# Second attention's loop in a decoder layer: another order of the PSUM banks and of GpSimd's work between its scatters

## The reference, cut to what matters

```
x = LN(x + linear_attention(x))             # 16 heads, elu + 1
x = LN(x + cross_attention(x, ctx_1024))    # 77 context rows a sequence, one head
x = LN(x + ffn(x))
```

```
h = x + proj(attention(LN1(x)))             # "second attention"
z = LN2(h)
gate = softmax(z @ router.T);  top_probs, top_idx = top_k(gate, 2)
out = h + sum over the token's two experts of top_prob * gelu(z @ w1[e]) @ w2[e]
```

## Time and profile before

| what | value |
|---|---|
| plain runs | 758.51, 765.23, 766.54 us; median 765.23 us |
| the profiled execution | 768.66 us, its span 766.9 us |
| busy share of the span | PE 85%, DVE 69%, ACT 51%, POOL 40% |
| mean granted clock of TensorE | 0.922 |

### The profile page before, as it was taken

One profiled execution on the slowest core, in us unless ns is written; L12 is line 12 of the kernel. 1 busy time (PEld: TensorE's weight loads), 2 busy tenths in 40 slices (PEclk: granted clock), 3 DMA queues, 4 the chain that ended last, 5 costly groups with the idle time before them and its releaser, 6 DMA issues.

```text
span 766.9 us, 19226 instructions
## 1 busy us (share of the span) xinstructions
PE 650.8 (85%) x5188; PEld 543.5 (71%) x5189; DVE 530.9 (69%) x1852; ACT 388.7 (51%) x921; POOL 309.5 (40%) x439
## 2 busy tenths in 40 slices
PE   6899999999962889888865319999999999999890
PEld 4679989988841667766655218888888888888540
DVE  1358788788752766888875757777777777777482
ACT  1345656666536656655543605555555555555143
POOL 0246776776631002566658731222222222322141
PEclk9899999999975999999976558999999999999995
DMA  6334434434311000111112331222222222222864
GB/s 203 90 106 130 134 92 141 135 96 119 99 22 28 2 3 2 44 57 57 52 49 71 111 99 50 71 81 69 72 80 69 73 79 69 76 76 63 318 233 133
DMA packets 47709, 68.13 MB, mean 89 GB/s; under 512 B 10576, under 2 KB 34512, under 8 KB 47664
## 3 DMA queue, kind: packets, MB, share of 16 engines
q1 hardware_dynamic: 39080, 46.01, 20.2%
q0 software_dynamic: 6480, 17.87, 6.3%
q10 hardware_dynamic: 2104, 3.68, 1.6%
HBM read 40.21 MB, written 23.12 MB: 83 GB/s over the span
## 4 chain that ended last, share of the span: by engine, by line
PE 54%; DVE 15%; issue 9%; POOL 8%; ACT 4%; DMA 2%; another core or an unknown queue 1%; SPq 1%; POOLq 0%; DVEq 0%; ACTq 0%
PE half_bank L145 9%; PE half_bank L147 9%; PE half_bank L146 9%; PE half_bank L1947 5%; PE half_bank L1475 3%; POOL at_rstd L456 3%; PE half_bank L1928 2%; PE half_bank L1399 2%; PE at_p_q_s L784 1%; POOL shared_x_lo L461 1%; DVE region_prob L1267 1%; DVE ba_top L1264 1%; DVE region_en_small L155 1%; DVE region_h_rows L1289 1%; PE at_p_kv L145 1%
## 5 line engine op out<-in xcount | busy, mean ns | idle before, releaser
L1755 POOL DMA_INDIRECT results<-all_w_qkv,ex_home x71 | 68.2, 960 | 212.3 <-DVE all_w_qkv L1891 183.3
L1788 ACT ACTIVATE region_hid_hi<-half_bank 128x256 fp32r<-128x256 f32 x142 | 46.9, 381 | 79.6 <-PE half_bank L1947 79.5
L145 PE MATMUL half_bank<-region_w_hi,region_hid_hi 128*128 x284 | 81.5, 287 | 1.1 <-DVE region_hid_lo L1883 1.1
L969 POOL DMA_INDIRECT dispatched<-all_xh,all_slot_u x64 | 66.6, 1040 | 36.0 <-DVE all_slot_u L1341 19.0
L146 PE MATMUL half_bank<-all_w,region_hid_hi 128*128 x284 | 79.9, 281 | 0.0
L147 PE MATMUL half_bank<-region_w_hi,region_hid_lo 128*128 x284 | 79.6, 280 | 0.0
L1891 DVE TENSOR_SCALAR all_w_qkv<-half_bank,ex_gate 128x256 f32<-128x256 f32 x71 | 34.3, 484 | 48.0 <-PE half_bank L147 47.5
L1775 ACT ACTIVATE all_xh<-half_bank,all_ln_b,all_ln_w 128x128 f32<-128x128 f32 x142 | 57.7, 466 | 19.5 <-PE half_bank L1928 19.5
L145 PE MATMUL half_bank<-region_w_hi,region_x_hi 128*128 x142 | 63.0, 444 | 0.5 <-DVE region_x_lo L1876 0.5
L1782 ACT ACTIVATE all_w_proj<-half_bank 128x512 f32<-128x512 f32 x71 | 42.5, 598 | 40.2 <-PE half_bank L147 40.2
L145 PEld LDWEIGHTS half_bank<-region_w_hi,region_hid_hi 128*128 128x128 f32 x284 | 53.4, 188 | 11.9 <-issue 8.9
(11 more groups left out here) (258 smaller groups left out, 1822.6 us busy)
## 6 DMA issues: line engine op xcount, KB each, us to landing
all_xh<-dispatched SPq DMA_DIRECT2D x71, 130.5 KB
all_w<-in_moe_w_dram SPq DMA_DIRECT2D x32, 256.0 KB, 3.1
region_y_first<-results SPq DMA_DIRECT2D x12, 512.0 KB, 10.7
all_resid<-at_x SPq DMA_DIRECT2D x32, 128.5 KB
shared_x_t<-in_x_t_dram SPq DMA_DIRECT2D x16, 256.0 KB, 4.2
at_x_tok<-in_x_dram SPq DMA_DIRECT2D x16, 256.0 KB, 4.2
out_dram<-all_w ACTq DMA_DIRECT2D x4, 512.0 KB
ck_ctx_t<-in_ctx_t_dram SPq DMA_DIRECT2D x4, 308.0 KB, 7.2
```

The costliest lines, as they stand in the source:

```text
L145: nc.tensor.matmul(out, a_hi, b_hi, start=(start and i == 0), stop=False)
L969: nc.gpsimd.indirect_dma_start(out=dram["dispatched"], out_offset=bass.IndirectOffsetOnAxis(ap=keep["slot_u"][g % SENDS][:, u, k:k + 1], a ...
L1755: nc.gpsimd.indirect_dma_start(out=dram["results"], out_offset=bass.IndirectOffsetOnAxis(ap=home[par][:, 0:1], axis=0), in_=ym[par], in_of ...
L1788: nc.scalar.activation(hid_hi[par][:, cs, :], p_t[half], ACT.Copy).then_inc(s["hid_high"], 1)
```

## The change

The list of the banks puts the queries before kv, and x before p. `send_rows` and `scatter` take numbers 0 to 7 (tile and expert together) in place of tiles. GpSimd's turn becomes: wait until the second bank of this turn's scores is full, five scatters, residual, one scatter, root, two scatters. What follows the last turn is unchanged but for the numbers.

```diff
-def send_rows(nc, dram, keep, g, tiles):
-
-    for u in tiles:
-        for k in range(2):
+def send_rows(nc, dram, keep, g, numbers):
+
+    for number in numbers:
+        for u, k in (divmod(number, 2),):
             nc.gpsimd.indirect_dma_start(
...
     for n in range(-2, GROUPS + 1):
-        for what, g, parts in (("s", n, 2), ("kv", n + 1, 1), ("q", n + 1, 2), ("p", n, 2), ("x", n + 2, 2), ("o", n, 2),
+        for what, g, parts in (("s", n, 2), ("q", n + 1, 2), ("kv", n + 1, 1), ("x", n + 2, 2), ("p", n, 2), ("o", n, 2),
                                ("v", n + 1, 2), ("a", n, 2), ("h", n - 1, 2)):
...
-        def scatter(g, tiles):
+        def scatter(g, numbers):
             wait_apart(pool, s["slots_ready"], g + 1)
-            send_rows(nc, dram, keep, g, tiles)
+            send_rows(nc, dram, keep, g, numbers)
...
         for n in range(1, GROUPS):
             if there(n - 3):
-                scatter(n - 3, range(0, 3))
-            root(n - 1)
+                bank_of.wait_full(pool, "s", n, 1)
+                scatter(n - 3, range(0, 5))
             residual(n - 1)
             if there(n - 3):
-                scatter(n - 3, range(3, NI))
-        scatter(GROUPS - 3, range(0, 3))
+                scatter(n - 3, range(5, 6))
+            root(n - 1)
+            if there(n - 3):
+                scatter(n - 3, range(6, 2 * NI))
+        scatter(GROUPS - 3, range(0, 6))
         root(GROUPS - 1)
-        scatter(GROUPS - 3, range(3, NI))
-        scatter(GROUPS - 2, range(NI))
-        scatter(GROUPS - 1, range(NI))
+        scatter(GROUPS - 3, range(6, 2 * NI))
+        scatter(GROUPS - 2, range(2 * NI))
+        scatter(GROUPS - 1, range(2 * NI))
         residual(GROUPS - 1)
```

## The result

The changed kernel took 761.39 us (median, 759.62 to 765.58) where the kernel before took 764.72 us in the same series: a ratio of 0.9968, 95% interval [0.9953, 0.9983]. The medians of the 20 runs each lie 3.3 us apart. The ratio with its interval is the measure used here, and by it the change is worth 2.4 us, 1.3 to 3.6 us. The forecast was 5.8 us less (759.4 us). The sign and the range were right, the size was not.

A forecast was written before the change was run, and what follows sets the result against it. A chain of waits was taken to bound each turn of the second attention's loop, with a late release to ScalarE in turns with scatters. 765.23 - (1.1 + 0 + 0.7 + 0.2 + 3.8 + 0 = 5.8) = 759.4 us; range 755.0 to 768.0.

The forecast's parts named there:

- Turn 0 and the banks: Second attention's loop, turn 0: outputs no longer wait for VectorE to free the kv bank, 1.1 us gained.
- The residual: GpSimd's adds leave VectorE's compares, 1.9 us of stretch per turn, for keys and values; worth nearly nothing alone.
- Root: GpSimd's root, which waits for VectorE's variance, just fits in the new order: cost 0, at most 0.5 us.
- Turns 4 to 6, 1.27 us each: Release of TensorE's turned probabilities to ScalarE follows the scatter train, so comes 1.27 us sooner per turn; 3.8 us.
- The rule that the release comes 0.6 us behind the last scatter: Turn 5: the late release before ScalarE's copy comes 0.6 us after the last of six back-to-back scatters.
- The release that stays where it is: Rival: late release unmoved, turns 4 to 6 give nothing; 2.0 us gained, 763.2 us; chance 0.35 with the do-nothing rival.
- That of the kv bank: Rival: delay comes from TensorE standing before the kv bank, new banks end it; 7.9 us gained, 757.3 us; chance 0.2.
- That of a release that waits for the sixth scatter: Rival: release waits for the sixth scatter, 2.4 us later in turns 3 to 6; plus 7.8 us, 773.0 us; chance 0.1.
- Turn 3, 0.2 us: Turn 3: gains 0.2 us, since the scores of turn 4 come no earlier than the h path allows.
- Turn 2, 0.7 us: Turn 2: TensorE's 0.59 us bank wait goes and compares are unstretched, until the scores are next; 0.7 us.
- let a turn shrink by 1.95 us: The h path, from statistics and root to the scores, lets a turn shrink by no more than about 1.95 us.
- The sum: All turns of the second attention's loop together: 5.8 us less than 765.23 us, giving 759.4 us.

The follow-up runs named there:

- a_banks: The kernel before with only the new order of the banks, GpSimd's program unchanged; ratio 0.9974 [0.9947, 1.0001] to the kernel before.
- f: The changed kernel with four scatters, residual, root, then four scatters; ratio 1.0145 [1.0097, 1.0194] to the kernel before.
- e: The changed kernel with all eight scatters behind root, residual first; ratio 1.0197 [1.0162, 1.0231] to the kernel before.
- i_all_behind_again: The changed kernel with eight scatters behind root, residual waiting for VectorE's probabilities, on a chip with late releases; 794.41 us, kernel before 765.42 us.
- after_again: The changed kernel without an edit, profiled again on a chip without late releases; ratio 0.9974 [0.9950, 0.9998] to the kernel before.
- i_all_behind: The changed kernel with eight scatters behind root, residual waiting for VectorE's probabilities, without late releases; ratio 1.0050 [1.0024, 1.0076] to the kernel before.

## Why the prediction was partly wrong

**Turn 0 and the banks: right.** 1.16 us were gained for 1.1 us forecast, the outputs start at 262.21 us, 9.6 us after the scores, and a_banks shows that it is the banks alone.

**The residual: right, and cheaper than it could have been.** The compares fell to 0.29 us and their sum to 0.19 us, and the keys and values kept 1.28 us. What I didn't see is what the place is worth: f and e, which start it 1.7 and 3.3 us sooner in turn 5, lose 11 and 15 us. The five scatters ahead of it serve as its delay.

**Root: right.** It starts at 360.62 us, 0.17 us behind the end of VectorE's variance.

**Turns 4 to 6, 1.27 us each: the step that failed.** Its first half held in the sum: the release came 1.63, 1.36 and 0.70 us sooner, 3.7 us together, where 3.8 us were forecast. But the step took the release for the only place where scatters hold TensorE up, and then put the sixth scatter, at no cost, over the outputs. Its working for turn 5 should have had two terms more: from the first to the last matmul the outputs are 0.43 us longer, and ScalarE's copy begins 0.90 us behind the start of the last of them instead of 0.26 us. 1.36 - 0.43 - 0.64 = 0.29 us; the three turns gave 0.52 + 0.29 + 0.08 = 0.89 us for 3.8 us. The row of ScalarE's copy in the kernel before:

```profile
365.39 1.08 ACT L1173 ACTIVATE region_o_t<-half_bank 128x512 f32<-128x512 f32 x2
```

In turn 6 the copy of the outputs was still 0.54 us sooner; the rest was lost behind it. The changed kernel has 6.8 us at the lower clock there (376.4 to 383.2 us), the kernel before 3.4 us (383.9 to 387.3 us). What share of the loss that has is not shown. The holes were measured; that one mechanism makes both the late releases and the holes is inferred: both come in the same executions, and i_all_behind_again moves TensorE's stops with the scatters.

The trace of the kernel before already had the sign, and the prediction didn't use it. In turn 4 the scores have a hole of 0.42 us at a place without any handshake, and a scatter from 330.34 to 331.31 us lies over their start. The hole begins 1 us behind the scatter's start, as those in the outputs do:

```profile
330.47 0.86 PE L1425 MATMUL half_bank<-region_k_diag,region_q_t 64*64 64x64 f32 x37
331.75 0.68 PE L1425 MATMUL half_bank<-region_k_diag,region_q_t 64*64 64x64 f32 x27 [0.42 <-issue]
```

These scores took 1.74 us from the first to the last matmul instead of 0.94 us. In the changed kernel they are whole, so part of the 0.52 us of turn 4 may be theirs.

The rule that the release comes 0.6 us behind the last scatter was read from turn 5 alone. In turn 6 of the kernel before, the copy begins 0.09 us before the sixth scatter ends (at 382.82 us), and in turn 3 it begins 0.68 us before:

```profile
382.73 1.33 ACT L1157 ACTIVATE region_prob_t<-half_bank 128x512 f32<-128x512 f32 x2 [3.05 <-remote]
```

So the late releases go with the scatters, but not at a fixed distance from the train's end.

**The rivals.** The release that stays where it is fell: it moved in turns 4 to 6. That of the kv bank fell: the outputs don't take this bank any more, and the copy still began 10.2 to 10.4 us after the scores in turns 3 to 6, not at 8.90 us. That of a release that waits for the sixth scatter fell too: in turn 5 the copy began at 357.22 us and the sixth scatter at 359.19 us.

**Turn 3, 0.2 us: wrong.** The outputs began 0.26 us sooner and ended 0.85 us later, with 55 matmuls in 1.46 us and a hole of 0.41 us, and the turn lasted 0.67 us longer.

**Turn 2, 0.7 us: wrong.** TensorE's wait for the bank went, but it wasn't what held the turn. The next scores come behind the h transposes, and these wait for ScalarE's rows, which wait for the root. The rows start 14.83 us after the scores in both kernels. ScalarE's rows and the h transposes in the changed kernel, and ScalarE's rows in the kernel before (its scores start at 292.17 us):

```profile
302.54 2.08 ACT L1117 ACTIVATE all_xh<-region_h_rows,ba_shift_h,ba_rstd_h 128x256 f32<-128x256 f32 x4 [0.92 <-POOL ba_shift_h L1062]
...
304.67 1.09 PE L1390 MATMUL half_bank<-all_identity,all_xh 128*128 128x128 f32 x8 [0.66 <-ACT all_xh L1117]
```

```profile
307.00 2.07 ACT L1114 ACTIVATE all_xh<-region_h_rows,ba_shift_h,ba_rstd_h 128x256 f32<-128x256 f32 x4 [0.68 <-POOL ba_shift_h L1062]
```

The same path holds the later turns where nothing is late (the wait of 1.31 us in after_again). No turn with scatters was shorter than 19.40 us in any run, and the 19.3 us forecast for turn 5 lie under that. The prediction let a turn shrink by 1.95 us; turn 5 could give at most 1.2 us.

**The sum.** In the profiled pair the loop gained 1.1 us, against 2.4 us (1.3 to 3.6) by the ratio. Without late releases the profiled loops went from 191.03 us (chip C) to 188.69 us (C), 189.65 and 188.77 us (D). One pair of executions can't tell 1.1 us from 2.4 us, and I leave the rest open.

**What stays open**: what part of the machine makes TensorE stand under the scatters, why on A and E and not on B, C and D, whether it belongs to the chip or to the moment (D was used twice, each other chip once), and whether four scatters ahead of the residual would do better there.

## What to carry to other kernels

When a long GpSimd elementwise instruction reads SBUF, look for the VectorE instructions with two SBUF inputs first: the same 2.3 us residual cost nothing over the keys and values, 1.9 us of slack over the compares, and 11 to 15 us of the kernel's time over the softmax. Before taking a delay's end as movable, ask what the agent of the delay will lie over next: here a scatter taken from the handshake was laid over the matmuls, and most of the gain was gone. And when a stall bears no name but "remote" or "issue" (or that of an engine that was long done, as the 1.63 us put down to TensorE in turn 5 of the changed kernel), look at the same program on a second chip before building a forecast on it.

## What the runs showed of the hardware that was not expected

Chip E, and A, which may be the same chip, show late releases and holes in TensorE's issue while GpSimd's indirect scatters run; B, C and D show neither for the same programs. This goes with about 11 us in the kernel before (764.72 and 765.42 against 753.39 to 754.16 us). Under eight scatters in a row 64 independent matmuls took 7.4 to 8.5 us instead of 0.94 us, the middle ones in pieces of one to five with 0.2 to 1.2 us between them, while VectorE's, ScalarE's and GpSimd's own instructions kept their durations (i_all_behind_again against i_all_behind, 0.03 us apart at most). The long matmuls of the two projections showed no hole (3.72 to 3.73 us and 5.40 us in turns 3 to 6 of the changed kernel on E, as in turns 1 and 2).

A VectorE product of two SBUF inputs that began 0.17 us after the first of two GpSimd adds was held until both were done, 2.72 us instead of 0.69 us (f_four_first).
